# The next pass's expert routing gathered into fewer job slots in passes 1 and 2 of a two-layer expert kernel

## The chip, the cores and the metric

The kernel runs on one core of a Trainium2 chip. The metric is the device time of one execution in microseconds, as the median of several runs. Five engines work side by side, each through its own list of instructions in order, and wait for each other by semaphores: TensorE (PE), VectorE (DVE), ScalarE (ACT), GpSimd (POOL) and SyncE (SP, which only issues transfers here).

## The reference, cut to what matters

```python
x = x + attention(layernorm(x))          # 4 batches x 512 tokens x 128
x = x + experts(layernorm(x))            # expert layer 1
x = x + recurrent(layernorm(x))          # gated linear recurrence, convolutions of 4 taps
x = x + experts(layernorm(x))            # expert layer 2, same weights

def experts(x):                          # 2048 tokens, 8 experts, 128 -> 352 -> 128
    scores = softmax(x @ gate_w.T)
    sel = top_k(scores + expert_bias, 2)             # two experts for each token
    for each (token, expert): row = x[token] * scores[token, expert]
        out[token] += (silu(row @ w1[e]) * (row @ w3[e])) @ w2[e]
```

Which expert a token goes to must be worked out on the chip before its rows can be gathered by expert. This working out is called routing here.

## The kernel before

**Passes and jobs.** After the attention, both expert layers run as one stream of 92 jobs on all engines. The 2048 tokens are cut in two halves of 1024, so there are four passes: pass 0 and 1 are layer 1 on the first and the second half of the tokens, pass 2 and 3 are layer 2 on the same halves. A pass (`m` in the code) has `JOBS` = 23 jobs; a job is up to 128 gathered rows of one expert. Job `J` = 23 m + s stands in slot `s` of pass `m`; jobs 23 to 45 are pass 1, jobs 46 to 68 pass 2, jobs 69 to 91 pass 3.

**One job.** POOL fetches 128 rows by an indirect DMA (`gather_pool`, L1482, "fetch" below). PE turns them (L1538), ACT copies them out of PSUM (L1550, "copy"), PE multiplies them with w1 (L1568, into bank A) and w3 (L1571, into one of two banks B); these two are "the product" of the job below. ACT takes the silu of bank A (L1642), DVE multiplies it with bank B (`mix_vector`, L1709, "mix"), PE turns the result (L1534), ACT copies it, PE multiplies with w2 (L1584), ACT takes the result out (`take_out_scalar`, L1649, "take-out"), and POOL scatters it to DRAM (`return_pool`, L1490, "return"). The stages are staggered: in the slot of job J, PE does the product of J, turns the mix of J-1 and the rows of J+2, and multiplies J-2 with w2; ACT takes out J-2.

**Waits between neighbours.** There is one bank A: `up_tensor(J)` waits for the silu of J-1 (`s_silu`). Everything that stands ahead of that silu in ACT's list so delays PE's next product.

**What is done between the jobs.** After its part of the job of a slot, each engine does what a table gives that slot (`between_tensor`, `between_scalar`, `between_vector`, `between_pool`): adding the results of the pass before, norms, the recurrence, and the routing of the next pass, m+1. The table for passes 1 and 2 is `IN_LATER`, made by `later(first, scale)`, which adds `first` (3 in pass 1, 1 in pass 2) to each entry. The routing of pass m+1 consists of these stages:

- `logits`: PE, 16 small products (L1285). `softmax`: DVE takes the maximum and subtracts it (L1343, L1344). `exp`: ACT (L1308), with a table load before it and another before the next silu.
- `top`: DVE, sum, reciprocal, scaling, bias (L1347 to L1350). `first`, `second`: DVE, six instructions each, the first and the second expert of each token (L1355 to L1363); `second` ends with `chosen` and lets PE go on with `ranks`.
- `weigh`: DVE, the weights of the chosen experts (L1365, L1366). `ranks`: PE, two products with `chosen` (L1291, L1292), which wait for `second`.
- `slots`: DVE, nine instructions (L1373 to L1382), wait for `ranks`. `spread`: DVE, eight instructions (L1386 to L1397); ACT then does its part (`high`, L1311), which waits for the seventh of them, `injob`.
- `scale`: ACT, in two parts of eight instructions (L1320), the tokens times their weights; SP stores each part (L1469). The first waits for `weigh`. Where ACT has `high` and `scale` in one slot, `high` stands ahead.
- `lanes`: DVE, two instructions (L1403). `number`: PE, 16 products (L1300). `ids`, `experts`: DVE, the lists by which POOL fetches and by which PE picks the weights of a job.

Entries of `JOBS` = 23 or more are done behind the last job of the pass, up to `LAST_SLOT`.

**Behind the last job.** PE turns and multiplies what is left of the last jobs, ACT takes it out, POOL returns it. The fetches of pass 2 stand in POOL's list behind the return of the last job of pass 1 (job 45), nine at once; those of pass 3 begin behind the return of job 66, whose take-out stands in slot 22 (job 68) of pass 2, and alternate with the returns. When all returns of a pass have landed, SP loads the results back (`yb`, L1503, two transfers of 512 KB for passes 0 and 1 each), for the sums of the layer.

The order on an engine is the order of the calls; in a slot the job comes first and the routing behind it:

```python
def job_vector(J):
    ...
    mix_vector(J)
    between_vector(m, s)
```

Of the kernel before, what the change touches and what calls it, by code (L numbers as in the profile page):

```python
# [28 lines left out]
JOBS = 23  # L29
# [36 lines left out]
def build(nc, x, W, Wi, Wf, Wg, conv_i, conv_f, gnw, Wo, gate_w, ebias, w1, w2, w3, out):  # L66
# [8 lines left out]
    with ExitStack() as ctx:  # L75
# [175 lines left out]
        first = sb("first", [P, NE])  # L251
# [981 lines left out]
        def later(first, scale):  # L1233
            at = {'add x': (0, 1), 'stats x': (1, 2), 'apply x': (2, 3), 'turn x': (3, 4), 'project': (4, 6), 'taps': (4, 6),
                  'conv f': (4, 7), 'tanh': (5, 8), 'conv i': (5, 8), 'gate': (5, 8), 'silu': (6, 9), 'recur': (6, 9),
                  'squares': (7, 10), 'finish': (8, 10), 'means': (8, 10), 'out': (10, 11),
                  'stats y': (10, 12), 'apply y': (11, 13), 'turn y': (12, 14),
                  'logits': 15, 'softmax': 15, 'exp': 15, 'top': 16, 'first': 16, 'second': 17, 'ranks': 18, 'weigh': 17,
                  'scale': scale, 'slots': 18, 'spread': 19, 'lanes': (19, 20), 'number': 20, 'ids': 20, 'experts': 20,
                  'root x': (-2, -1), 'rms': (6, 8), 'root y': (8, 10)}  # L1240
            return {k: tuple(n + first for n in slots) if type(slots) is tuple else slots + first for k, slots in at.items()}

        IN_LATER = {1: later(3, (17, 18)), 2: later(1, (18, 19))}
        LAST_SLOT = {0: JOBS, 1: 24, 2: JOBS, 3: JOBS}
        ADDS_IN_LAST = (4, 5)


# [304 lines left out]
        experts = {}  # L1552
# [35 lines left out]
        def job_tensor(J):  # L1588
# [16 lines left out]
            if s == JOBS - 1:  # L1605
                turn_tensor_step(m, JOBS)
                down_tensor(J - 1)
                down_tensor(J)
                for s in range(JOBS, LAST_SLOT[m]):
                    between_tensor(m, s)  # L1610

        def between_tensor(m, s):
# [4 lines left out]
            elif m < 3:  # L1617
                at = IN_LATER[m]
                for k in range(2):
# [31 lines left out]
        def job_scalar(J):  # L1651
# [10 lines left out]
            if s == JOBS - 1:  # L1662
                turn_scalar_step(m, JOBS)
                take_out_scalar(J - 1)
                take_out_scalar(J)
                for s in range(JOBS, LAST_SLOT[m]):
                    between_scalar(m, s)

        def between_scalar(m, s):
# [4 lines left out]
            elif m < 3:  # L1674
                at = IN_LATER[m]
                for k in range(2):
# [46 lines left out]
        def between_vector(m, s):  # L1723
# [8 lines left out]
            elif m < 3:  # L1732
                at = IN_LATER[m]
                for k in range(2):
# [171 lines left out]
        def between_pool(m, s):  # L1906
# [3 lines left out]
            if m in (1, 2):  # L1910
                at = IN_LATER[m]
                for k in range(2):
# [166 lines left out]
```

## Time and profile before

| | |
|---|---|
| device time, median of 3 runs | 536.09 us (532.87 to 545.83) |
| span of the profiled execution | 534.2 us |
| PE, DVE, ACT, POOL busy in it | 427.9, 330.9, 333.2, 310.0 us |
| returns (L1490) on POOL | 92, 93.5 us busy, 52.4 us idle before them for ACT's take-out |
| mixes (L1709) on DVE | 92, 47.8 us busy, 83.8 us idle before them for PE's product |
| turns of fetched rows (L1538) on PE | 92, 10.8 us idle before them for the fetch |

Times in the trace count from the span's start. A row of a timeline has the start, the time on the engine, the line, the operation and its operands, and in brackets how long the engine was idle before it and what ended that. A row of a table of stretches has the stretch, its length, the busy time of each engine with the number of its instructions, and the granted clock of TensorE (1.00 is its upper level, 0.50 its lower).

### The profile page before, as it was taken

The numbers are of one execution on the slowest core, as the hardware profiler recorded it, in microseconds if no ns is written. First come the engines' busy times: TensorE is split into PE (matmuls) and PEld (weight loads), VectorE is DVE, ScalarE is ACT, GpSimd is POOL, SyncE is SP. The second block draws the span as 40 slices with busy tenths as digits, with TensorE's granted clock in tenths as the row PEclk, the third lists the DMA queues.
The fourth block names the chain that finished last, engine by engine and source line by source line (L and its number), as shares of the span: only waits on it lengthen the run. The fifth ranks groups of instructions, "written<-read, shape, count | busy, mean of one in ns | idle before, by whom it ended". The sixth has DMA issues, their size and how long they took to land. (4 is left out here: it accounts for less than half of the span.)

```text
span 534.2 us, 11420 instructions
## 1 busy us (share of the span) xinstructions
PE 427.9 (80%) x3805; PEld 321.2 (60%) x3822; DVE 330.9 (62%) x799; ACT 333.2 (62%) x624; POOL 310.0 (58%) x333
## 2 busy tenths in 40 slices
PE   3777798778787766998798798975799895699990
PEld 2455576556565554786576567753577774477770
DVE  5988889969957887154641678547377757132112
ACT  2486699899895868556754275564366565255550
POOL 5345385764663338676457576724567752667771
PEclk9796899999998679899999799897799998999996
DMA  7344353273369411112311312103311222151324
GB/s 156 82 110 92 89 115 74 79 141 55 88 158 293 100 42 42 41 45 43 113 41 49 109 50 37 34 21 117 106 34 44 38 40 95 36 162 51 56 51 128
DMA packets 36371, 43.50 MB, mean 81 GB/s; under 512 B 5876, under 2 KB 31276, under 8 KB 36292
## 3 DMA queue, kind: packets, MB, share of 16 engines
q1 hardware_dynamic: 30428, 30.70, 22.3%
q0 software_dynamic: 5888, 12.07, 9.2%
q8 instruction: 34, 0.56, 0.4%
q14 instruction: 21, 0.17, 0.1%
HBM read 25.91 MB, written 15.86 MB: 78 GB/s over the span
## 5 line engine op out<-in xcount | busy, mean ns | idle before, releaser
L1490 POOL DMA_INDIRECT token_out<-ysb,id_out x92 | 93.5, 1016 | 75.3 <-ACT ysb L1649 52.4
L1139 POOL TENSOR_TENSOR PP<-PP,E 128x512 f32<-128x512 f32 x64 | 83.1, 1299 | 72.9 <-ACT PP L1092 72.8
L1709 DVE TENSOR_TENSOR hid<-silu,ps 128x352 f32<-128x352 f32 x92 | 47.8, 519 | 114.6 <-PE ps L1571 83.8
L1092 ACT ACTIVATE PP<-A,feps 128x1024 f32<-128x1024 f32 x80 | 93.0, 1163 | 20.8 <-DVE A L1024 20.8
L1024 DVE TENSOR_SCALAR A<-ps 128x1024 int32<-128x1024 int32 x80 | 96.0, 1219 | 15.3 <-PE ps L923 14.0
L1482 POOL DMA_INDIRECT tiled<-scaled_rows,id_in x92 | 89.7, 975 | 26.7 <-issue 21.5
L1550 ACT ACTIVATE turned<-ps 128x512 f32<-128x512 f32 (+2 forms) x104 | 56.9, 547 | 67.8 <-PE ps L1538 63.7
L1568 PE MATMUL ps<-room,turned 128*128 x184 | 75.9, 495 | 11.4 <-ACT silu L1642 9.3
L1584 PE MATMUL ps<-room,turned 128*128 x552 | 79.8, 281 | 3.5 <-ACT ysb L1649 3.1
L1584 PEld LDWEIGHTS ps<-room,turned 128*128 128x128 f32 x552 | 70.8, 196 | 5.6 <-issue 5.2
L1571 PE MATMUL ps<-room,turned 128*128 x184 | 72.5, 477 | 0.0
L1642 ACT ACTIVATE silu<-ps 128x352 f32<-128x352 f32 x92 | 42.5, 462 | 38.6 <-PE ps L1568 38.5
L923 PE MATMUL ps<-QS,KS 102*128 102x128 bf16 (+2 forms) x448 | 53.6, 259 | 12.6 <-DVE A L1024 10.2
L1534 PEld LDWEIGHTS ps<-ident,hid 128*128 128x128 f32 x276 | 36.9, 146 | 28.8 <-issue 20.1
L923 PEld LDWEIGHTS ps<-QS,KS 102*128 102x128 bf16 x448 | 34.2, 105 | 27.5 <-DVE A L1024 11.2
L1534 PE MATMUL ps<-ident,hid 128*128 128x128 f32 x276 | 47.2, 282 | 3.5 <-DVE hid L1709 3.5
L1571 PEld LDWEIGHTS ps<-room,turned 128*128 128x128 f32 x184 | 36.3, 197 | 21.2 <-issue 2.8
L1101 ACT ACTIVATE E<-ps 128x512 f32<-128x512 f32 x64 | 38.4, 600 | 3.7 <-PE ps L953 3.6
L1568 PEld LDWEIGHTS ps<-room,turned 128*128 128x128 f32 x184 | 29.4, 199 | 16.4 <-issue 16.2
L1538 PE MATMUL ps<-ident,tiled 128*128 128x128 f32 x92 | 26.6, 289 | 12.1 <-DMA tiled<-scaled_rows,id_in 10.8
L1649 ACT ACTIVATE ysb<-ps 128x128 f32<-128x128 f32 x92 | 25.5, 277 | 15.0 <-PE ps L1584 10.5
L194 POOL TENSOR_TENSOR lnr<-lnv,mhalf 128x4 f32<-128x4 f32 x16 | 17.3, 1080 | 19.3 <-DVE lnv L188 19.3
(223 smaller groups left out, 640.9 us busy)
## 6 DMA issues: line engine op xcount, KB each, us to landing
parts<-room SPq DMA_DIRECT2D x32, 128.0 KB, 2.4
scaled_rows<-xT SPq DMA_DIRECT2D x8, 512.0 KB, 2.7
yb<-token_out SPq DMA_DIRECT2D x8, 512.0 KB, 4.2
QS<-parts SPq DMA_DIRECT2D x21, 192.0 KB
KS<-parts SPq DMA_DIRECT2D x21, 192.0 KB
room<-in_L_ffn_w_dram SPq DMA_DIRECT2D x2, 1408.0 KB, 8.1
tiled<-scaled_rows,id_in POOLq DMA_INDIRECT x92, 2.7
token_out<-ysb,id_out POOLq DMA_INDIRECT x92, 2.4
```

The lines of the kernel that those rows point to most:

```text
L923: return pe.matmul(bank[:, col:col + width], KS[:, slot, h, P * j:P * j + P], QS[:, slot, h, t0:t0 + width], start=True, stop=True)
L1024: v.tensor_scalar(A[:, U % 3, :].bitcast(I32), ps[:, bank:bank + 2, :].rearrange("p k t -> p (k t)").bitcast(I32), 0x7fffffff, None, ALU.b ...
L1092: a.activation(PP[:, G % 2, 2 * p:2 * p + 2, :].rearrange("p k t -> p (k t)"), A[:, U % 3, :], ACT.Square, bias=feps[:, G // NG:G // NG + ...
L1139: g.tensor_tensor(w, w, E[:, hh % 4, :], MUL).then_inc(s_PD, 1)
L1482: g.indirect_dma_start(rows[:, J % ROWS, :], None, xs_d[m], bass.IndirectOffsetOnAxis(ap=id_in[:, m % 2, s:s + 1], axis=0)).then_inc(s_row ...
L1490: g.indirect_dma_start(yr_d[m], bass.IndirectOffsetOnAxis(ap=id_out[:, m % 2, s:s + 1], axis=0), ysb[:, J % OUTS, :], None).then_inc(s_ret ...
L1534: ins = pe.transpose(ps[:, BK_R, P * c:P * c + P], hid[:, J % 2, P * c:P * c + P], ident[:, :])
L1550: a.activation(turned[:, n % 2, c0:c1, :].rearrange("p c l -> p (c l)"), ps[:, BK_R, P * c0:P * c1], ACT.Copy).then_inc(s_t, 1)
L1568: pe.matmul(ps[:, BK_A, 0:HID], turned[:, n % 2, 3, :], w13[:, bass.ds(e, 1), 0, :].squeeze(1), start=True, stop=True).then_inc(s_AB, 1)
L1571: pe.matmul(ps[:, BK_B + J % 2, 0:HID], turned[:, n % 2, 3, :], w13[:, bass.ds(e, 1), 1, :].squeeze(1), start=True, stop=True).then_inc(s_ ...
L1584: ins = pe.matmul(ps[:, BK_Y, 0:P], turned[0:hw, n % 2, c, :], w2s[0:hw, bass.ds(e, 1), c, :].squeeze(1), start=(c == 0), stop=(c == len(H ...
L1709: v.tensor_tensor(hid[:, J % 2, 0:HID], silu[:, J % 2, :], ps[:, BK_B + J % 2, 0:HID], MUL).then_inc(s_hid, 1)
```

## The change

In `IN_LATER` the stages of the routing stand in other slots. Slots of the job stream, with `first` added:

| stage | pass 1, before | pass 1, now | pass 2, before | pass 2, now |
|---|---|---|---|---|
| logits, softmax, exp | 18 | 18 | 16 | 16 |
| top, first | 19 | 18 | 17 | 16 |
| second, weigh | 20 | 19 | 18 | 17 |
| ranks | 21 | 19 | 19 | 17 |
| slots | 21 | 20 | 19 | 18 |
| spread, high | 22 | 20 | 20 | 18 |
| scale, two parts | 20, 21 | 20, 21 | 19, 20 | 18, 19 |
| lanes, two parts | 22, 23 | 21, 21 | 20, 21 | 19, 19 |
| number, ids, experts | 23 | 22 | 21 | 20 |

Nothing is left for slot 23 of pass 1, so its `LAST_SLOT` falls from 24 to 23. No instruction is added or removed, and the lists of POOL and SP are the same.

```diff
-                  'logits': 15, 'softmax': 15, 'exp': 15, 'top': 16, 'first': 16, 'second': 17, 'ranks': 18, 'weigh': 17,
-                  'scale': scale, 'slots': 18, 'spread': 19, 'lanes': (19, 20), 'number': 20, 'ids': 20, 'experts': 20,
+                  'logits': 15, 'softmax': 15, 'exp': 15, 'top': 15, 'first': 15, 'second': 16, 'ranks': 16, 'weigh': 16,
+                  'scale': scale, 'slots': 17, 'spread': 17, 'lanes': (18, 18), 'number': 19, 'ids': 19, 'experts': 19,
...
-        IN_LATER = {1: later(3, (17, 18)), 2: later(1, (18, 19))}
-        LAST_SLOT = {0: JOBS, 1: 24, 2: JOBS, 3: JOBS}
+        IN_LATER = {1: later(3, (17, 18)), 2: later(1, (17, 18))}
+        LAST_SLOT = {0: JOBS, 1: JOBS, 2: JOBS, 3: JOBS}
```

The first place is DVE in pass 1 behind the mix of job 41: the difference of the two lists, where L1343 and L1344 are the softmax stage, L1709 is the mix of job 42, and L1347 begins the stage `top`.

```order
 L1343 TENSOR_REDUCE m1<-ps 128x8
 L1344 TENSOR_TENSOR L8<-ps,m1 128x64
-L1709 TENSOR_TENSOR hid<-silu,ps 128x352
 L1347 TENSOR_REDUCE m1<-L8 128x8
 L1348 RECIPROCAL m1<-m1 128x8
```

The mix of job 42 now stands behind the stages `top` and `first`, ten instructions later in the list; pass 2 has the same difference at job 63.

The second place is PE around the `ranks` products (L1291, L1292) of pass 1. Before, they stood behind the w2 product of job 42 and ahead of the product of job 45, the last of the pass; the rows are those two and what follows them:

```order
 L1291 MATMUL ps<-chosen,trib 128x64
 L1292 MATMUL ps<-chosen,onesb 128x64
 L1568 ISA
 L1568 MATMUL ps<-room,turned 128x352
 L1571 ISA
 L1571 MATMUL ps<-room,turned 128x352
```

Now they stand behind the w2 product of job 40 (the rows L1584) and ahead of the product of job 43, whose `chosen` DVE works out in the same slot:

```order
L1584 MATMUL ps<-room,turned 128x128
L1291 MATMUL ps<-chosen,trib 128x64 [waits s_rd,s_M]
L1292 MATMUL ps<-chosen,onesb 128x64
L1568 ISA [waits s_silu,s_t]
L1568 MATMUL ps<-room,turned 128x352
```

So two whole jobs of PE (43 and 44) now stand behind these products that stood ahead of them.

The third place is ACT in pass 1 from the take-out of job 41 in slot 20 on: L1320 is a part of `scale`, L1642 the silu, L1311 the part `high`. Before:

```order
L1649 ACTIVATE ysb<-ps 128x128
L1320 ACTIVATE xT<-xh,wts 128x128 x8
L1642 ACTIVATE silu<-ps 128x352
L1550 ACTIVATE turned<-ps 128x384
L1649 ACTIVATE ysb<-ps 128x128
L1320 ACTIVATE xT<-xh,wts 128x128 x8
L1642 ACTIVATE silu<-ps 128x352
L1550 ACTIVATE turned<-ps 128x384
L1649 ACTIVATE ysb<-ps 128x128
L1311 ACTIVATE injobid<-injob,idhi 128x16x23
```

Now:

```order
L1649 ACTIVATE ysb<-ps 128x128
L1311 ACTIVATE injobid<-injob,idhi 128x16x23
L1320 ACTIVATE xT<-xh,wts 128x128 x8
L1642 ACTIVATE silu<-ps 128x352
L1550 ACTIVATE turned<-ps 128x384
L1649 ACTIVATE ysb<-ps 128x128
L1320 ACTIVATE xT<-xh,wts 128x128 x8
L1642 ACTIVATE silu<-ps 128x352
```

The part `high` has moved from behind both parts of `scale` and the silu of job 45 to ahead of the first part and of the silu of job 44. In pass 2 `high` stood ahead of the second part of `scale` and now stands ahead of the first.

## Rows read from the trace of the kernel before

**Rows 1.** Timeline of ACT, pass 1, slots 18 to 22 (start, us, instruction, idle before)
```profile
348.32 1.28 ACT L1308 ACT_TABLE_LOAD   x1
350.23 0.26 ACT L1308 ACTIVATE L<-L 128x64 f32<-128x64 f32 x1 [0.63 <-DVE L L1344]
...
357.79 2.44 ACT L1320 ACTIVATE xT<-xh,wts 128x128 f32<-128x128 f32 x8 [2.42 <-DVE wts L1366]
360.13 0.44 ACT L1642 ACTIVATE silu<-ps 128x352 f32<-128x352 f32 x1
...
363.34 0.45 ACT L1642 ACTIVATE silu<-ps 128x352 f32<-128x352 f32 x1
...
366.38 0.63 ACT L1311 ACTIVATE injobid<-injob,idhi 128x368 bf16<-128x368 bf16 x1 [1.16 <-DVE injob L1395]
...
368.74 0.28 ACT L1649 ACTIVATE ysb<-ps 128x128 f32<-128x128 f32 x1 [1.21 <-PE ps L1584]
```

**Rows 2.** Timeline of DVE, pass 1, slots 19 to 22
```profile
352.73 0.21 DVE L1347 TENSOR_REDUCE m<-L 128x8 f32<-128x64 f32 x1
...
355.29 0.52 DVE L1709 TENSOR_TENSOR hid<-silu,ps 128x352 f32<-128x352 f32 x1
...
357.00 0.23 DVE L1363 TENSOR_TENSOR chosen<-oh 128x64 bf16<-128x64 f32 x1
...
360.66 0.52 DVE L1709 TENSOR_TENSOR hid<-silu,ps 128x352 f32<-128x352 f32 x1 [2.91 <-ACT silu L1642]
...
363.18 0.27 DVE L1382 TENSOR_TENSOR base<-ps,cumE 128x64 f32<-128x64 f32 x1
...
364.32 0.29 DVE L1386 TENSOR_TENSOR Q<-oh,base 128x128 f32<-128x128 f32 x1
...
365.80 0.54 DVE L1395 TENSOR_TENSOR injob<-iojob,jobof 128x368 bf16<-128x368 f32 x1
```

**Rows 3.** Timeline of PE, products and ranks of pass 1
```profile
352.50 0.85 PE L1568 MATMUL ps<-room,turned 128*128 x2 [0.44 <-ACT silu L1642]
353.19 0.76 PE L1571 MATMUL ps<-room,turned 128*128 x2
...
354.89 0.76 PE L1568 MATMUL ps<-room,turned 128*128 x2
...
357.28 0.20 PE L1291 MATMUL ps<-chosen,trib 128*128 128x64 bf16 x1
...
360.82 1.54 PE L1568 MATMUL ps<-room,turned 128*128 x2 [3.30 <-ACT silu L1642]
```

**Rows 4.** Table of stretches: busy time of each engine, granted clock, DMA
```profile
357.40:360.70 3.30, 0.12 (x2) 0.00 (x0) 0.35 (x3) 2.92 (x10) 0.00 (x0) 1.00 0.03 6
360.80:364.10 3.30, 3.28 (x8) 2.18 (x9) 2.59 (x11) 3.00 (x11) 0.97 (x1) 0.50 0.45 179
```

**Rows 5.** Timeline, from pass 1 to pass 2: POOL, SP, PE
```profile
369.30 0.97 POOL L1490 DMA_INDIRECT token_out<-ysb,id_out  x1 [0.40 <-ACT ysb L1649]
371.19 0.98 POOL L1482 DMA_INDIRECT tiled<-scaled_rows,id_in  x1 [0.92 <-DVE id_in L1413]
...
371.80 0.80 SPq L1503 DMA_DIRECT2D yb<-token_out  x2
...
376.04 0.45 PE L1538 MATMUL ps<-ident,tiled 128*128 128x128 f32 x1 [6.42 <-DMA tiled<-scaled_rows,id_in]
```

**Rows 6.** Timeline, from pass 2 to pass 3: ACT, POOL, PE
```profile
433.24 0.26 ACT L1308 ACTIVATE L<-L 128x64 f32<-128x64 f32 x1 [0.63 <-DVE L L1344]
...
456.28 0.28 ACT L1649 ACTIVATE ysb<-ps 128x128 f32<-128x128 f32 x1 [0.79 <-PE ps L1584]
...
456.83 0.97 POOL L1490 DMA_INDIRECT token_out<-ysb,id_out  x1 [4.73 <-PE ps L1534]
458.11 0.98 POOL L1482 DMA_INDIRECT tiled<-scaled_rows,id_in  x1 [0.31 <-issue]
...
460.83 0.30 PE L1538 MATMUL ps<-ident,tiled 128*128 128x128 f32 x1 [1.61 <-DMA tiled<-scaled_rows,id_in]
```

## The prediction

> **What bounds the kernel now.** I first read the page for the share of each engine: none is full, PE is busiest with 80% of the span, so the job stream loses its time in waits and each stretch has to be read by itself. I then read the timelines of ACT, DVE and PE for slots 18 to 22 of pass 1 and 16 to 22 of pass 2, the only places that the change touches, and the waits of POOL and PE behind the last jobs.
>
> In [rows 1 to 3] the routing of pass 1 is seen to set the pace. The product of job 45 begins at 360.82, after PE was idle for 3.30 us [rows 3]. It waited for the silu of job 44 at 360.13, which stands in ACT's list behind the first part of `scale`, and that waited 2.42 us for the weights from DVE [rows 1]. The granted clock is 1.00 in that idle stretch and 0.50 in the next one, 2.4 and then 1.2 GHz [rows 4]; the first half of the product takes 1.54 us in place of 0.85 [rows 3].
>
> Between the passes the chain goes over transfers. The take-out of job 45 is at 368.74 [rows 1], its return at 369.30, and the fetch of job 46 only at 371.19, of which 0.92 us is a wait for the list `id_in` [rows 5]. PE can turn the fetched rows at 376.04, 4.85 us after the fetch began. The same step from pass 2 to 3 takes 2.72 us (458.11 to 460.83) [rows 6]. What differs is that SP begins to load 2 x 512 KB of results at 371.80, 0.61 us behind the fetch [rows 5].
>
> **What the change does to this.** I work out the new times in pass 1 from the instructions' own times, with before in brackets.
>
> 1. *Softmax to first choice.* Until the exponential, nothing moves: it ends at 350.49 [rows 1]. `top` and `first` then take 355.29 - 352.73 = 2.56 us on DVE [rows 2], so the mix of job 42 stands at 353.1. I price its own delay, about 0.8 us against a silu that ends near 352.3, at nothing as such, because PE turns it only in its next slot. What counts is what follows.
>
> 2. *`ranks` two jobs earlier.* `second` ends 357.23 - 355.29 = 1.94 us after the mix before it starts [rows 2], so at 355.0. PE has nothing left from 352.06 (the product at 352.50 less its 0.44 us idle) [rows 3]. The two `ranks` products stand ahead of the product of job 43 and are waited for now, where two jobs of work covered them before. With 0.05 us to begin and 0.2 us for them [rows 3], this product begins at 355.3 (352.50): **2.8 us late**. Queued behind it are the w2 product of job 41, its take-out and its return, and on DVE the mix of job 43, which needs bank B: 1.45 us after the product begins (353.19 + 0.76 - 352.50) [rows 3], at 356.75.
>
> 3. *`slots` and `spread` together, `high` ahead of `scale`.* From the mix to the end of `slots` it is 363.45 - 360.66 = 2.79 us, and to the end of `injob` another 366.34 - 364.32 = 2.02 us [rows 2]: 361.55. ACT waits for that with `high`, then 0.63 us for `high` and 2.34 us (360.13 - 357.79) for the first part of `scale` [rows 1]. The silu of job 44 begins at 364.5 (360.13): **4.4 us late**. PE is done with its work of the slot by about 360.1 (2.39 us for a job [rows 3], begun at 357.7) and idle until 365.1, again long enough for the lower clock, as before. The weights themselves are ready early now, which gains nothing, since `high` is ahead of their reader in the list.
>
> 4. *End of pass 1.* The silu of job 45 follows 3.21 us later (363.34 - 360.13) [rows 1], at 367.7 (363.34). `lanes` are done by then on DVE. Before, ACT's list still had `high` ahead of the last copies, and 5.40 us lay between this silu and the last take-out (368.74 - 363.34) [rows 1]. Now mix, turn, copy, w2 product and two take-outs follow in about 4.5 us: 372.2. That is **3.5 us late**, so four fifths of the 4.4 us remain.
>
> 5. *The fetch.* `ids` are long done, and the 0.92 us wait for them goes. The return of job 45 starts 0.56 us after its take-out and takes 1.27 us of POOL with the gap (458.11 - 456.83) [rows 5, 6]: the fetch starts at 374.0 (371.19), 2.8 us late. SP's loads begin 2.50 us after the start of the return (371.80 - 369.30) [rows 5], so 1.2 us behind the fetch now in place of 0.61. I take it that the fetch then keeps ahead of them and needs 2.72 us as in [rows 6], not 4.85 us. It may still need all of that; both ends go into the range. PE turns the rows at 376.75 (376.04): **0.7 us late**.
>
> 6. *Pass 2.* The list is the same one shifted by 433.24 - 350.23 = 83.01 us [rows 1, 6], up to the silu of job 65 at 447.5 and that of 66 at 450.7. The product of job 66 begins at 448.1 at the lower clock and lasts about 2.8 us (twice 1.45); with 1.4 us for the rest of the slot and 0.5 us for `number` the product of 67 begins at 452.8, that of 68 2.4 us later, and the take-out of 66 another 2.5 us behind: 457.7 (456.28), **1.4 us late** [rows 6]. The first fetch of pass 3 stands right behind the return of 66, so it is late by as much; it never waited for the lists, so their earlier slot gives nothing.
>
> The sum is 0.7 + 1.4 = 2.1 us on the profiled execution's 534.2 us, which gives 536.3. That execution lies 1.9 us below the median of the runs shown, 536.09, so I put the same 2.1 us on the median: **538.2 us**, 0.4% longer. Bounds: each of the two `ranks` waits leaves PE idle for some 3 us. If the clock falls to the lower level just as the late product begins, that costs the second 1.45 us of it [rows 3, 4]; both times, +2.9 us. If the fetch still needs 4.85 us, +2.1 us. Against this, if PE's idle time soaks up half of either delay, -1.8 and -0.7 us.
>
> Two rules of the Trainium skill can be held against these rows. The trace has the exponential 1.91 us after its table load began, and the 0.63 us idle before it was for DVE [rows 1]. The Trainium skill, page "ScalarE: Activation LUTs", section "What ACT_TABLE_LOAD costs", counts 1.28 us for the load and 1.38 us more for a drain, 2.66 us for each switch. By it the exponential could not begin before 350.98 and step 1 would end 0.75 us later in each pass; the trace, with the exponential at 350.23, does not agree. The other is on step 5. In the trace the same fetch takes 4.85 us with the loads 0.61 us behind it and 2.72 us without them [rows 5, 6]. The Trainium skill, page "DMA: Bandwidth & Descriptors", section "Queues, rings and completion order", says that a DMA engine takes turns between the queues that have work. By it the loads slow every fetch that is under way, whichever began first, and most of the 2.1 us would not come back; the trace shows a fetch slowed that began first, so this counts as a rival below.
>
> **Rivals.**
>
> - *The boundary pays for it (faster).* At the turn from pass 1 to 2 the change takes away 0.92 us of waiting for `id_in` and up to 2.13 us (4.85 - 2.72) of the fetch [rows 5, 6], 3.05 us in all. If the last take-out is late by less than 3.05 us the turn gains; if it is not late at all, because DVE's stages now fill time in which PE waited for ACT anyway (3.30 us idle at 360.82 [rows 3]), the kernel takes 536.1 - 3.05 = 533.0 us. For it: second choice and weights end 2.2 us sooner on DVE. Against it: `high` now holds ACT for `spread`.
> - *Clock and crowding (slower).* The waits of steps 2 and 3 come at the lower clock and the fetch stays slow: 538.2 + 2.9 + 2.1 = 543.2 us at most, 541 us with about half. For it: one idle stretch of this size in pass 1 has the clock at 0.50 right behind it [rows 4]. The rule on the DMA queues above is part of this case.
> - *Hidden anyway.* The late jobs wait for the same fetches and returns in the end, and only noise is left: 536.1 us. Against it: in the turn to pass 2 the fetches stand behind the last return in POOL's list, so the delay has no buffer to go into.
>
> **How the numbers follow.** The forecast, 536.5 to 540 us, has 0.45; clock and crowding, 540 to 543.5 us, 0.25; faster at the turn, 532.5 to 535.5 us, 0.2; hidden, around 536, 0.1. The range that leaves out no more than 2 in 10 reaches from 533.5 to 543.5 us. The two percent that a measurement of this kernel can tell from no change is 10.7 us; no case reaches it, and only the scatter of the runs (532.87 to 545.83) or something unseen would. So: faster 0.04, same 0.88, slower 0.08.
>
> **What would show it.** In the changed kernel's timeline PE should idle about 3 us before the `ranks` products in both passes; ACT should wait for `injob` (L1311) about 3 us before the first part of `scale`; POOL's 0.92 us for `id_in` should be gone; the first fetch of pass 2 should take under 3.5 us until PE turns it. Wrong would be the forecast if the last take-out of pass 1, measured from the exponential, comes less than 20.5 us behind it (18.5 before, 22.0 forecast), or if the first fetch takes over 4 us.

## The result and the profile after

The changed kernel takes 545.16 us (median of 4 runs, 543.99 to 545.28) against 537.38 us of the kernel before (4 runs, 532.87 to 545.83): ratio 1.0153, 95% interval 1.0116 to 1.019, so 7.8 us slower. Forecast were 538.2 us and a range up to 543.5 us. The direction came true and both waits are there; the size did not, and neither did what was said of the turn between the passes and of the clock. The forecast started from 536.09 us, the median of three runs; with a fourth the kernel before is at 537.38 us. Beside that the change cost 7.8 us, where 2.1 us were forecast.

The span of the profiled execution is 543.5 us (534.2 before). 1.3 us of that difference is there before the first moved instruction: the exponential of pass 1 ends at 351.79 and not at 350.49 [rows 1]. I therefore read everything from that exponential on. First the timeline of ACT in slots 18 to 22 of pass 1 (columns as before), which answers to [rows 1].

```profile
351.53 0.26 ACT L1308 ACTIVATE L<-L 128x64 f32<-128x64 f32 x1 [0.63 <-DVE L L1344]
...
357.47 0.46 ACT L1642 ACTIVATE silu<-ps 128x352 f32<-128x352 f32 x1 [3.25 <-PE ps L1568]
...
363.05 0.62 ACT L1311 ACTIVATE injobid<-injob,idhi 128x368 bf16<-128x368 bf16 x1 [2.62 <-DVE injob L1395]
363.57 2.42 ACT L1320 ACTIVATE xT<-xh,wts 128x128 f32<-128x128 f32 x8
365.89 0.44 ACT L1642 ACTIVATE silu<-ps 128x352 f32<-128x352 f32 x1
...
369.10 0.45 ACT L1642 ACTIVATE silu<-ps 128x352 f32<-128x352 f32 x1
...
372.96 0.28 ACT L1649 ACTIVATE ysb<-ps 128x128 f32<-128x128 f32 x1 [1.21 <-PE ps L1584]
```

ACT now waits 3.25 us for the late product of job 43 and 2.62 us for `injob` ahead of `scale`. From the exponential to the silu of job 44 it is 14.4 us (9.9 before), to the last take-out 21.4 us (18.5). PE in the same slots and in the turn to pass 2, as the work between the last job of one pass and the first of the next is called below, answering to [rows 3, 5]:

```profile
356.38 0.20 PE L1291 MATMUL ps<-chosen,trib 128*128 128x64 bf16 x1 [3.01 <-DVE chosen L1363]
...
356.58 0.85 PE L1568 MATMUL ps<-room,turned 128*128 x2
...
366.58 0.85 PE L1568 MATMUL ps<-room,turned 128*128 x2 [3.60 <-ACT silu L1642]
...
377.58 0.45 PE L1538 MATMUL ps<-ident,tiled 128*128 128x128 f32 x1 [4.66 <-DMA tiled<-scaled_rows,id_in]
378.48 1.53 PE L1568 MATMUL ps<-room,turned 128*128 x2 [0.45 <-ACT turned L1550]
...
382.00 0.45 PE L1538 MATMUL ps<-ident,tiled 128*128 128x128 f32 x1 [0.81 <-DMA tiled<-scaled_rows,id_in]
```

Both new waits are there. The first of them is followed by a product at the upper clock (0.85 us); the clock falls 1.5 us later. The first fetch of pass 2 is turned at 377.58; the second, at 382.00, is a wait that the kernel before did not have. The transfers of the turn, POOL and SP:

```profile
373.51 0.97 POOL L1490 DMA_INDIRECT token_out<-ysb,id_out  x1 [0.52 <-ACT ysb L1649]
374.79 0.99 POOL L1482 DMA_INDIRECT tiled<-scaled_rows,id_in  x1 [0.30 <-issue]
376.08 0.97 POOL L1482 DMA_INDIRECT tiled<-scaled_rows,id_in  x1 [0.30 <-issue]
...
376.03 0.80 SPq L1503 DMA_DIRECT2D yb<-token_out  x2
```

The wait for `id_in` (0.92 us in [rows 5]) is gone and the first fetch starts 1.24 us ahead of the loads. The second is issued 0.05 us behind them. The trace gives for the first and for the second, from issue to landing:

```profile
DMA to landing us min/median/max: 2.7/2.7/2.7
...
DMA to landing us min/median/max: 5.8/5.8/5.8
```

Pass 2 and the turn to pass 3, PE and ACT, answering to [rows 6]:

```profile
438.07 0.26 ACT L1308 ACTIVATE L<-L 128x64 f32<-128x64 f32 x1 [0.62 <-DVE L L1344]
...
442.91 0.20 PE L1291 MATMUL ps<-chosen,trib 128*128 128x64 bf16 x1 [3.00 <-DVE chosen L1363]
...
443.11 1.40 PE L1568 MATMUL ps<-room,turned 128*128 x2
...
453.56 0.44 ACT L1642 ACTIVATE silu<-ps 128x352 f32<-128x352 f32 x1
...
454.24 1.54 PE L1568 MATMUL ps<-room,turned 128*128 x2 [4.61 <-ACT silu L1642]
...
464.57 0.28 ACT L1649 ACTIVATE ysb<-ps 128x128 f32<-128x128 f32 x1 [0.18 <-PE ps L1584]
```

Here the product behind the `ranks` wait runs at the lower clock: 1.40 us for its first half, 0.85 us in pass 1. The table of stretches (length; busy time of PE, PEld, DVE, ACT, POOL; granted clock) shows where the clock is low:

```profile
357.90:361.30 3.40, 3.40 (x14) 2.89 (x13) 2.74 (x11) 0.91 (x3) 0.60 (x1) 0.51 0.02 5
375.10:388.60 13.50, 9.39 (x19) 5.19 (x20) 2.33 (x4) 2.82 (x7) 8.27 (x9) 0.50 0.41 125
443.30:446.60 3.30, 3.30 (x10) 2.18 (x10) 0.75 (x4) 0.48 (x2) 0.00 (x0) 0.50 0.03 5
453.60:460.30 6.70, 6.06 (x32) 4.65 (x33) 3.80 (x7) 4.59 (x15) 2.24 (x2) 0.50 0.42 168
470.60:477.40 6.80, 6.25 (x16) 3.58 (x15) 1.04 (x2) 1.98 (x5) 4.49 (x5) 0.50 0.18 54
```

The same table of the kernel before:

```profile
371.10:381.20 10.10, 4.32 (x9) 2.27 (x10) 1.48 (x5) 1.30 (x4) 7.62 (x8) 0.50 0.45 150
381.40:449.40 68.00, 61.26 (x372) 47.09 (x371) 48.73 (x144) 43.53 (x96) 40.38 (x40) 1.00 0.17 43
449.60:456.30 6.70, 4.99 (x23) 3.88 (x24) 4.22 (x13) 1.48 (x5) 1.72 (x1) 0.50 0.22 88
456.40:524.00 67.60, 58.39 (x337) 43.94 (x335) 14.58 (x27) 32.52 (x76) 48.23 (x49) 1.00 0.27 72
```

So in the turn to pass 2 the lower clock lasts 3.4 us longer now, and the stretches at 443 and 470 us have no counterpart before. The idle time of 3.60 us ahead of the product at 366.58 was not followed by the lower clock: from 361.4 to 374.9 us it is 1.00.

The stretches below are differences of start times in one trace each; `after_again` and `after_third` are two later traces of the changed kernel. "exp" is the exponential of the pass, "s44" the silu of job 44, "y45" the take-out of job 45; the take-outs y45 and y66 are those that the first fetches of the next pass hang on.

| kernel | exp to s44 | s44 to y45 | y45 to s46 | s46 to s49 | sum | exp to s65 | s65 to y66 | y66 to s69 | s69 to s72 | sum |
|---|---|---|---|---|---|---|---|---|---|---|
| before | 9.9 | 8.6 | 9.8 | 7.1 | 35.4 | 5.5 | 17.6 | 6.3 | 7.8 | 37.1 |
| changed | 14.4 | 7.1 | 7.1 | 10.5 | 39.1 | 15.5 | 11.0 | 6.6 | 8.9 | 42.1 |
| changed, `after_again` | 14.4 | 8.7 | 7.1 | 9.8 | 40.0 | 15.6 | 9.8 | 7.1 | 9.9 | 42.5 |
| changed, `after_third` | 14.4 | 8.8 | 7.1 | 10.0 | 40.2 | 15.6 | 8.7 | 7.2 | 9.6 | 41.1 |

Between s49 and the exponential of pass 2 the first two traces take 47.6 and 47.5 us, from s72 to the last take-out 51.0 and 50.9 us. So the loss behind the first exponential is in these columns, 3.7 us in the sum of pass 1 and 4.9 us in that of pass 2; only some 0.4 us of it comes back behind the last take-out. The single columns of the three traces of the changed kernel differ by up to 2.3 us (s65 to y66), which is to be kept in mind wherever one trace is compared with another.

### The profile page after: what moved, and what is told of

It reads as the page before. It is cut to its first block and busy times, and to the rows that moved or that the text cites. A ratio compares the mean times of both kernels' runs of the same rounds, so it can differ in the third digit from the quotient of the medians.

```text
span 543.5 us, 11435 instructions
## 1 busy us (share of the span) xinstructions
PE 437.7 (81%) x3822; PEld 325.6 (60%) x3822; DVE 329.9 (61%) x799; ACT 333.2 (61%) x624; POOL 312.0 (57%) x333
## 5 line engine op out<-in xcount | busy, mean ns | idle before, releaser
L1490 POOL DMA_INDIRECT token_out<-ysb,id_out x92 | 94.6, 1028 | 82.0 <-ACT ysb L1649 62.0
L1709 DVE TENSOR_TENSOR hid<-silu,ps 128x352 f32<-128x352 f32 x92 | 47.7, 518 | 119.8 <-PE ps L1571 97.1
L1568 PE MATMUL ps<-room,turned 128*128 x184 | 78.8, 512 | 14.5 <-ACT silu L1642 12.5
L1584 PE MATMUL ps<-room,turned 128*128 x552 | 80.0, 282 | 2.5 <-ACT ysb L1649 2.2
L1571 PE MATMUL ps<-room,turned 128*128 x184 | 74.7, 490 | 0.0
L1584 PEld LDWEIGHTS ps<-room,turned 128*128 128x128 f32 x552 | 71.0, 196 | 4.3 <-issue 4.0
L1642 ACT ACTIVATE silu<-ps 128x352 f32<-128x352 f32 x92 | 42.5, 461 | 44.3 <-PE ps L1568 44.2
L923 PE MATMUL ps<-QS,KS 102*128 102x128 bf16 (+2 forms) x448 | 54.0, 260 | 11.2 <-DVE A L1024 8.8
L1534 PEld LDWEIGHTS ps<-ident,hid 128*128 128x128 f32 x276 | 36.8, 146 | 30.1 <-issue 20.8
L1571 PEld LDWEIGHTS ps<-room,turned 128*128 128x128 f32 x184 | 37.7, 205 | 22.6 <-issue 5.3
L1568 PEld LDWEIGHTS ps<-room,turned 128*128 128x128 f32 x184 | 30.3, 205 | 19.2 <-issue 18.9
L1101 ACT ACTIVATE E<-ps 128x512 f32<-128x512 f32 x64 | 38.4, 600 | 3.1 <-PE ps L953 2.9
L1649 ACT ACTIVATE ysb<-ps 128x128 f32<-128x128 f32 x92 | 25.5, 277 | 15.5 <-PE ps L1584 11.0
```

The lines of the kernel that those rows point to most:

```text
L923: return pe.matmul(bank[:, col:col + width], KS[:, slot, h, P * j:P * j + P], QS[:, slot, h, t0:t0 + width], start=True, stop=True)
L1490: g.indirect_dma_start(yr_d[m], bass.IndirectOffsetOnAxis(ap=id_out[:, m % 2, s:s + 1], axis=0), ysb[:, J % OUTS, :], None).then_inc(s_ret ...
L1534: ins = pe.transpose(ps[:, BK_R, P * c:P * c + P], hid[:, J % 2, P * c:P * c + P], ident[:, :])
L1568: pe.matmul(ps[:, BK_A, 0:HID], turned[:, n % 2, 3, :], w13[:, bass.ds(e, 1), 0, :].squeeze(1), start=True, stop=True).then_inc(s_AB, 1)
L1571: pe.matmul(ps[:, BK_B + J % 2, 0:HID], turned[:, n % 2, 3, :], w13[:, bass.ds(e, 1), 1, :].squeeze(1), start=True, stop=True).then_inc(s_ ...
L1584: ins = pe.matmul(ps[:, BK_Y, 0:P], turned[0:hw, n % 2, c, :], w2s[0:hw, bass.ds(e, 1), c, :].squeeze(1), start=(c == 0), stop=(c == len(H ...
```

## The experiments

My theory was: PE's waits for `ranks` and for the silu behind `high`, with the lower clock that they bring, make the loss (A). Rivals: it is made in the turn, by SP's loads ahead of the second fetch (B); only `high` ahead of `scale` counts (C) or only `ranks` (D). The experiments ran on three chips. On two of them (chips 7 and 13) the kernel before takes 537.4 and 537.6 us, as in the first comparison, whose chip is not known. On chip 6 it takes 570 to 573 us; no trace of it was kept there, but every kernel traced there takes longer outside the routing (52.4 to 56.2 us from s49 to the exponential of pass 2). Ratios are to the kernel before on the same chip, with 95% intervals. The stretches can be compared over chips in part: with the old table in pass 1, `pass2_only` on chip 6 has 9.9, 8.6, 9.8 and 7.1 us as the kernel before has above, and `exp to s44` of the changed kernel is 14.4 us in all its traces; where the lower clock plays in, they scatter by 1 to 2 us.

**Undoing one list edit each.** `ranks_later`:

```diff
-'second': 16, 'ranks': 16, 'weigh': 16,
+'second': 16, 'ranks': 17, 'weigh': 16,
```

> The changed kernel with one entry put back: ranks stands one slot behind second again, all other stages stay where the change put them. Theory A (PE's waits, and the lower clock behind them, make the loss; changed kernel 545.2 us): the 3.0 us idle time ahead of L1291 goes in both passes, the mixes of jobs 43 and 64 come 1.2 to 2.5 us sooner, and the granted clock no longer falls right behind that wait; about 541 us. Rival B (the loss is made in the turn from pass 1 to 2, where SP's 2 x 512 KB loads stand ahead of the second and third fetch): the turn still costs its 3.5 us, only the direct 1.2 us of each pass come back; about 543 us. Rival C (only the lists' order on ACT counts, high ahead of scale): no more than 1 us, 544 us.

Measured on chip 6: 1.0051 (1.0007 to 1.0095), 575.1 us beside 572.5 us, near the 541 us of theory A.

`high_later` leaves the table and moves ACT's part one slot later and behind `scale`:

```diff
-            if s == at["spread"]:
-                prepare_scalar(m + 1, "high")
             for k in range(2):
                 if s == at["scale"][k]:
                     scale_scalar(m + 1, k)
+            if s == at["spread"] + 1 and m:
+                prepare_scalar(m + 1, "high")
```

> The changed kernel, only ACT's part high (L1311) of passes 1 and 2 moved to the slot behind, after the second part of scale, so that the silu of jobs 44 and 65 no longer waits for injob. Theory A: the silu of jobs 44 and 65 comes about 3 us sooner, PE's idle time of 3.60 and 4.61 us ahead of the next product falls to 1 to 2 us; 2.5 to 3 us come back in each pass, about 539.5 us. Rival B: the delay of the last take-out shrinks, but the second fetch of pass 2 is still behind the loads; about 541 us. Rival D (the ranks wait alone is what counts, and high is hidden by it): 544 to 545 us.

Measured: 0.9974 (0.9927 to 1.0022), 573.1 us. `both_later` has both:

> The changed kernel with both edits: ranks one slot later, and high behind scale in the slot behind. Theory A: both waits gone, about 536 us, level with the kernel before or 1 us below it. Rival B: the turn from pass 1 to 2 still costs 3 us, about 539 us.

Measured: 0.9936 (0.9884 to 0.9989), 567.5 us; repeated on chip 13 as `both_later_2`:

> The changed kernel with ranks one slot later and high behind scale, as both_later, now beside the others on one chip. By its stretches 3.2 us better than the kernel before in passes 1 and 2 together, ratio 0.992 to 0.996; so 9 to 12 us better than the changed kernel. If the two list edits only trade with the clock, 0.998 or more.

Measured: 0.9893 (0.9857 to 0.9929), 531.9 us beside 537.6 us, and 12.8 us below the changed kernel on that chip, somewhat more than expected. The stretches:

| kernel | exp to s44 | s44 to y45 | y45 to s46 | s46 to s49 | sum | exp to s65 | s65 to y66 | y66 to s69 | s69 to s72 | sum |
|---|---|---|---|---|---|---|---|---|---|---|
| ranks_later | 13.0 | 8.7 | 7.1 | 10.1 | 38.9 | 13.0 | 10.7 | 7.0 | 8.1 | 38.7 |
| high_later | 11.4 | 7.6 | 7.0 | 10.0 | 36.0 | 12.3 | 9.2 | 7.1 | 8.0 | 36.6 |
| both_later | 7.7 | 10.7 | 7.1 | 10.4 | 35.9 | 8.6 | 10.2 | 7.2 | 7.4 | 33.4 |
| both_later_2 | 7.7 | 10.7 | 7.1 | 10.6 | 36.0 | 7.7 | 10.7 | 7.1 | 9.3 | 34.7 |

`exp to s44` falls by 1.4, 3.0 and 6.7 us, `exp to s65` by 2.5, 3.2 and 6.9 to 7.8 us: both waits are real, each is partly hidden behind the other, and in these stretches the two together are worth more than their sum. In the times they are not: against the changed kernel on chip 6 (1.0127) they gain 0.8%, 1.5% and together 1.9%, with intervals of 0.5% each. That `high_later` alone is level with the kernel before excludes D. C is excluded less firmly: `ranks_later` lies 0.8% below the changed kernel, just beyond the noise, and its take-outs y45 and y66 come 1.4 and 1.7 us nearer to the exponentials than in the trace of the changed kernel on that chip; of the two, `high` ahead of `scale` weighs more. `high_later` came out much better than the 539.5 us that I had expected by theory A, level with the kernel before. In the timeline of ACT of `both_later_2` one sees why the pair wins:

```profile
349.94 0.26 ACT L1308 ACTIVATE L<-L 128x64 f32<-128x64 f32 x1 [0.63 <-DVE L L1344]
...
355.28 2.45 ACT L1320 ACTIVATE xT<-xh,wts 128x128 f32<-128x128 f32 x8 [0.20 <-DVE wts L1366]
357.64 0.44 ACT L1642 ACTIVATE silu<-ps 128x352 f32<-128x352 f32 x1
...
358.51 2.44 ACT L1320 ACTIVATE xT<-xh,wts 128x128 f32<-128x128 f32 x8
360.84 0.62 ACT L1311 ACTIVATE injobid<-injob,idhi 128x368 bf16<-128x368 bf16 x1
```

The weights are ready when ACT comes to `scale` (0.20 us of waiting, 2.42 us in [rows 1]), and `high` finds `injob` done.

**The stage that the change is named for, alone.** `top_first_only` is the kernel before with `top` and `first` moved into the logits' slot:

```diff
-'top': 16, 'first': 16,
+'top': 15, 'first': 15,
```

> The kernel before with one part of the change alone: top and first moved into the slot of the logits, ahead of the mix of jobs 42 and 63; second, weigh, ranks and all later stages as before. In the traces this part by itself delays one mix by 0.8 us that PE does not need yet, and it makes the next mix 1.7 us sooner. If the waits for ranks and high make the loss, this part costs nothing: ratio to the kernel before 0.998 to 1.002, the silu of job 44 at most 0.3 us off. If the mix put behind DVE's ten instructions is what costs, 1 to 2 us slower and a later silu 44.

Measured on chip 7: 0.9957 (0.9912 to 1.0001), 536.6 us beside 537.4 us; exp to s44 is 8.7 us (9.9), 1.2 us less where 0.3 us at most was expected. The mix that DVE does later is not missed. The wait of DVE for the exponential ahead of the mix shows no cost; this part of the change is at worst neutral.

**The two passes apart.** `pass1_only` and `pass2_only` give the old entries to the other pass.

```diff
-        IN_LATER = {1: later(3, (17, 18)), 2: later(1, (17, 18))}
+        IN_LATER = {1: later(3, (17, 18)), 2: later(1, (18, 19), True)}
```

This is `pass1_only`, where `True` puts the old entries into the table; `pass2_only` has it the other way round, with the old `LAST_SLOT`.

> The new table in pass 1 alone, pass 2 as before. By the first traces the changed kernel loses 3.5 us up to slot 3 of pass 2 (the turn included) and 4.8 us from the routing of pass 2 on. So this one should be 3.5 us (2.5 to 4.5) slower than the kernel before. If the second fetch behind SP's loads is the main cause, most of the 8 us is here.

> The new table in pass 2 alone, pass 1 as before: 4.8 us (3.5 to 6) slower than the kernel before, no wait for SP's loads being involved. If the turn from pass 1 to 2 is the main cause, 1 to 2 us only.

> The changed kernel itself once more, beside the others on one chip, as the measure for them: ratio to the kernel before 1.012 to 1.019 if the first comparison holds on any chip; theory and rivals agree on it. If a chip with slower transfers hides the loss in its own waits, the ratio is below 1.01.

Measured on chip 6: 1.0141 (1.0092 to 1.019), 1.0054 (1.001 to 1.0099), and 1.0127 (1.007 to 1.0183) for the whole change; by the medians that is 6.9, 3.3 and 7.2 us. The two parts add up to more than the whole, within the intervals. It is not the split that I had expected (3.5 and 4.8 us), and by the times alone most of the loss is in pass 1, as rival B would have it. The stretches decide:

| kernel | exp to s44 | s44 to y45 | y45 to s46 | s46 to s49 | sum | exp to s65 | s65 to y66 | y66 to s69 | s69 to s72 | sum |
|---|---|---|---|---|---|---|---|---|---|---|
| pass1_only | 14.7 | 7.7 | 7.1 | 10.0 | 39.3 | 5.5 | 17.2 | 6.4 | 9.3 | 38.4 |
| pass2_only | 9.9 | 8.6 | 9.8 | 7.1 | 35.4 | 15.6 | 10.6 | 6.9 | 7.2 | 40.4 |

Pass 1 costs 3.9 us, and 3.8 us of that are there at the take-out of job 45. The turn behind it, y45 to s49, takes 17.0 us with the new table and 16.9 us with the old one. So the loss is not made in the turn: the turn only fails to give back what the prediction had counted on. Pass 2, which has no such loads, costs 2.0 us here (40.4 against 38.4), or 3.2 us against the kernel before. B is thereby excluded as the maker of the loss.

**The clock without the waits.** `fill_all` and `fill_waits` leave every wait and give PE products to do in it that nobody reads. The edit of `fill_waits`:

```diff
+        def fill_tensor(n):
+            for _ in range(n):
+                nc.tensor.transpose(ps[:, BK_F, 0:P], ident[:, :], ident[:, :])
...
+                    fill_tensor(26)
                 pe.wait_ge(s_M, m + 1)
...
+            if m in (1, 2) and s == IN_LATER[m]["spread"] + 2:
+                fill_tensor((0, 30, 38)[m])
```

> The changed kernel with turns of a constant tile on PE, into a PSUM bank that is free there, that nobody reads: 26 ahead of ranks, 28 ahead of the product of jobs 45 and 66, 38 ahead of the first fetched rows of pass 2 and 12 ahead of those of pass 3 (0.11 us each at the upper clock). They do no useful work and move no wait, they only keep PE busy. Theory A with the clock as the larger part: the granted clock stays at 1.00 in slots 19 to 22 of pass 1 and 17 to 20 of pass 2 and behind both turns, and 4 to 6 us of the 8 us come back, about 540 us. If the clock is only a by-product: no change or some tenths slower, 545 to 546 us.

Measured on chip 6: 1.0078 (1.0036 to 1.012). It settles nothing: its second filling stood one slot too early (`spread` + 1), and between the passes it had 38 more ahead of the fetched rows. There, from the take-out of job 45 to the silu of 46, it took 11.2 us in place of 7.1. So I made `fill_waits`, in the two waits alone:

> The changed kernel with PE kept busy by products that nobody reads in its two waits alone: 26 ahead of ranks in passes 1 and 2 (3.0 us of waiting there), 30 ahead of the product of job 45 and 38 ahead of that of job 66 (3.6 and 4.6 us of waiting there); nothing in the turns between the passes. No wait is moved. If the lower clock behind the waits is the larger part of the loss, 3 to 5 us come back against the changed kernel run beside it and the granted clock stays at 1.00 through these slots. If the waits alone count, the difference is under 1 us.

Measured on chip 6: 1.0097 (1.0056 to 1.0138) beside 1.0127 of the changed kernel, too close to tell. Repeated on chip 13 with more executions:

> The changed kernel once more beside the two below, with more rounds: 1.013 to 1.016 of the kernel before, whichever theory holds.

> The changed kernel with PE kept busy by products nobody reads in its two waits (as fill_waits). Earlier traces have it 1.6 us better than the changed kernel in pass 1 and 4.2 us in pass 2, the times only 0.3% (2.4 us less, intervals of 4 us). If the clock holds the larger part of the loss as those traces say: 4 to 6 us better than the changed kernel, ratio to before 1.003 to 1.008. If the clock is the smaller part: 1.009 to 1.012.

Measured: the changed kernel 1.014 (1.0106 to 1.0175), with fillings 1.0067 (1.0036 to 1.0098), 544.7 and 540.4 us. The difference of 0.0073 is 3.9 us, with the two intervals together uncertain by about 2.5 us; on chip 6 it was 0.003. So a part of the loss, by the better of the two measurements about half, is the clock behind the waits, and the rest is left with the clock mostly held up there. The timeline of PE in `fill_waits_2` (L1279 is the filling, L1576 the first half of the product):

```profile
354.76 0.20 PE L1299 MATMUL ps<-chosen,trib 128*128 128x64 bf16 x1 [0.16 <-DVE chosen L1371]
...
354.97 0.85 PE L1576 MATMUL ps<-room,turned 128*128 x2
...
359.55 3.44 PE L1279 MATMUL ps<-ident 128*128 128x128 f32 x30
364.98 0.85 PE L1576 MATMUL ps<-room,turned 128*128 x2 [1.99 <-ACT silu L1652]
```

The idle time ahead of `ranks` is 0.16 us in place of 3.01, and these products are at the upper clock. Beside the trace of the changed kernel on the same chip, `after_third`:

| kernel | exp to s44 | s44 to y45 | y45 to s46 | s46 to s49 | sum | exp to s65 | s65 to y66 | y66 to s69 | s69 to s72 | sum |
|---|---|---|---|---|---|---|---|---|---|---|
| after_third | 14.4 | 8.8 | 7.1 | 10.0 | 40.2 | 15.6 | 8.7 | 7.2 | 9.6 | 41.1 |
| fill_waits_2 | 14.4 | 7.7 | 7.1 | 10.0 | 39.1 | 14.4 | 8.7 | 7.0 | 7.7 | 37.8 |

The fillings give back 1.1 us in pass 1, ahead of the last take-out, and 3.3 us in pass 2, more than half of it not before the first jobs of pass 3 (s69 to s72). In pass 1 the lower clock lasts 3.2 us (366.2 to 369.4) in place of 6.6 us (369.4 to 376.0 in `after_third`); the turn to pass 2 runs at the lower clock for 13.4 or 13.5 us in both.

**The turn.** `hold_loads` is the changed kernel with SP's loads held back until PE has turned the third fetch:

```diff
+            if m == 1 and b % 2 == 0:
+                sp.wait_ge(s_tp, turns(2 * JOBS + 2))
             sp.dma_start(yb[:, b % 2], ...)
```

> The changed kernel, SP's two loads of pass 1's results (yb, 2 x 512 KB) held back until PE has turned the rows of job 48, the third fetch of pass 2; nothing else moved. If the loads ahead of the second and third fetch are the reason why job 46 to 49 took 10.0 to 10.5 us (silu of 46 to silu of 49) in place of 7.1 us, this falls by 1 to 2 us, though the sum with yb then comes later (its DVE part may give some of it back); 1 to 2 us better than the changed kernel. If only the lower clock is the reason, the stretch stays at 9.5 to 10.5 us.

Measured on chip 7: 1.0148 (1.009 to 1.0206), no gain. Silu of 46 to silu of 49 is 7.7 us where the three traces of the changed kernel have 9.8 to 10.5, so the loads did cost 2 to 3 us there. A part of that is clock: the lower level lasts 6.7 us in this turn (378.8 to 385.5) in place of 13.5. But the gain is given back: from s49 to the exponential of pass 2 it is 49.9 us in place of 47.5, since DVE now waits for the results that it adds and holds the mix behind them (timeline of DVE, the wait in brackets):

```profile
388.05 0.69 DVE L1511 TENSOR_TENSOR yb<-yb 128x512 f32<-128x512 f32 x1 [1.65 <-DMA yb<-token_out]
388.78 0.69 DVE L1512 TENSOR_TENSOR xt<-xt,yb 128x512 f32<-128x512 f32 x1
389.39 0.51 DVE L1711 TENSOR_TENSOR hid<-silu,ps 128x352 f32<-128x352 f32 x1
```

`early_two` moves two fetches in front instead, between the returns of jobs 44 and 45:

```diff
-            return (J - ROWS, max(17 + s // 2, J - 9), max(2 * JOBS - 1, J - 9), ...)[m]
+            return (J - ROWS, max(17 + s // 2, J - 9), 2 * JOBS - 2 if s < 2 else max(2 * JOBS - 1, J - 9), ...)[m]
```

> The changed kernel, and POOL issues the first two fetches of pass 2 between the returns of jobs 44 and 45, not behind that of 45: possible only because the lists are now ready by then. The first fetch starts about 1.5 us sooner, the loads 2.5 us later, three fetches land before the loads take the DMA engines. Last take-out of pass 1 to silu of job 49: 17.6 us in the changed kernel, 16.8 before; here 14.5 to 15.5 us, so 2 to 3 us better than the changed kernel. If the clock alone sets that stretch, 17 us and no gain.

Measured on chip 7: 1.0116 (1.0041 to 1.0191), not told apart from the changed kernel by its times, so the 2 to 3 us expected do not show there. In the trace y45 to s49 is 14.7 us (5.6 + 9.1) in place of 16.9 to 17.6, as expected, and s49 to the next exponential stays at 47.5: nothing given back. The same trace has 8.8 us from s44 to y45, where the lower clock lasts from 367.7 to 374.6 us; the first trace of the changed kernel has 7.1 us there at the upper clock, its two repetitions 8.7 and 8.8 us. So this term depends on where the clock falls in each run.

**All together.** `best` has both list edits, the two early fetches, and the fetches of pass 3 one return sooner (`3 * JOBS - 4` in place of `3 * JOBS - 3`).

> Both list edits (ranks one slot later, high behind scale) and the fetches issued sooner, the first two of pass 2 between the returns of 44 and 45 and those of pass 3 one return sooner. From the parts: the two list edits alone gave 0.9936 of the kernel before; the early fetches should give 2 to 3 us at the first turn and 1.5 us at the second. Ratio 0.984 to 0.990. If the turns are bound by the clock or by the loads anyway, 0.993 as without them.

Measured on chip 7: 0.9773 (0.9731 to 0.9815), 525.0 us (524.3 to 527.1) beside 537.4 us, 12 us faster than the kernel before and more than I had added up. Its stretches are 7.7, 9.6, 5.0, 8.9 (31.2) and 7.7, 10.7, 4.5, 7.3 (30.1). POOL in the turn to pass 2:

```profile
370.17 0.99 POOL L1482 DMA_INDIRECT tiled<-scaled_rows,id_in  x1 [0.30 <-issue]
371.46 0.96 POOL L1482 DMA_INDIRECT tiled<-scaled_rows,id_in  x1 [0.30 <-issue]
372.72 1.00 POOL L1490 DMA_INDIRECT token_out<-ysb,id_out  x1 [0.31 <-issue]
```

And the table of stretches of `best` from 4.1 us behind the silu of job 46 past the turn to pass 3:

```profile
379.50:461.00 81.50, 72.23 (x434) 54.58 (x433) 54.41 (x160) 49.36 (x111) 52.58 (x52) 1.00 0.19 53
```

The early fetches to pass 2 are possible only because the lists are ready before the last return; in the kernel before, POOL still waited for `id_in` behind it. Without them `both_later_2` was 1.1% faster than the kernel before, so the new table is worth having by itself once the two stages are moved. The clock holds its upper level from 379.5 us through the routing of pass 2 and the turn to pass 3, where the kernel before had 6.7 us of the lower one. `both_later_2`, without the early fetches, has the lower clock there again (456 to 466 us), and `early_two`, without the list edits, from 453 to 460 us; why the two together escape it is not shown.

## Why the prediction was wrong

- **Steps 1 and 2 held.** `ranks` was waited for 3.01 and 3.00 us; with the 1.3 us by which the traces differ beforehand taken off, the product of job 43 was 2.8 us late, as worked out, and in pass 2 the product of 64 began at 438.28 on the time axis of before (forecast 438.3).
- **Step 3 held.** The silu of job 44 was 5.76 - 1.3 = 4.5 us late (forecast 4.4).
- **Step 4 held in its sign.** The last take-out was 4.22 - 1.30 = 2.9 us late (forecast 3.5) in this trace; in the two repetitions of the changed kernel it comes 23.1 us behind the exponential, where before has 18.5, so 4.5 and 4.6 us late: nothing of the 4.4 us was soaked up there.
- **Step 5 is where it failed first.** It had the turn give back 2.8 us, from 3.5 us late at the take-out to 0.7 us late at the turned rows. The first fetch did escape the loads and landed in 2.7 us, as said, and its rows were turned 0.2 us late. But I priced the turn by the first fetch alone. The second, issued 0.05 us behind SP's loads, took 5.8 us and PE had to wait 0.81 us for it, and the lower clock lasted 3.4 us longer; before, the first fetch took that blow and the second, 5.1 us under way, landed while PE was busy with the first job. By s49 the loss was 3.7 us, not 0.7 us: from y45 to s49 it is 16.9 us before and 17.6, 16.9 and 17.1 us in the three traces of the changed kernel, so the turn gave nothing back. `hold_loads` shows the loads' share with the clock in it (2 to 3 us of that stretch), `early_two` that moving fetches ahead of them wins it without giving it back. The "2.13 us gained" was moved to the next fetch.
- **Step 6 failed in the clock.** The product of job 64 began when forecast and then ran at the lower clock: its mix came at 441.06 on the time axis of before, against 439.75 by the steps. I had that price, 1.45 us, in the bounds and left it out of the sum, though the mix behind it is in the chain. In this trace y66 was 3.5 us late (forecast 1.4), in the repetitions 2.4 and 1.3 us. From y66 to s72, which I had at nothing, another 1.4 us are lost here and 2.9 and 2.7 us in the repetitions; but two kernels with the scale and `ranks` of pass 2 where they were before, `pass1_only` and `top_first_only`, have 9.3 and 9.6 us from s69 to s72 as well, where the kernel before has 7.8 us in its one trace. So this last part can't be put down to the change with certainty.
- **The range.** Its upper end allowed 1.45 us of clock for each of two waits and 2.1 us for the fetch, 5.0 us in all. The measured 545.16 us lie 1.7 us above it, of which 1.3 us is the start value (536.09 us of three runs, 537.38 us of four). The case "clock and crowding" was the nearest one and had a quarter of the chance, but the fetch that it let stay slow was the first, and that one was fast.
- **The signs.** All that was named as a sign came true: the idle time ahead of `ranks`, ACT's wait for `injob` (2.62 us), no wait for `id_in`, the first fetch under 3.5 us, the take-out beyond 20.5 us. None of them looked at the second fetch or at the clock, where the forecast failed.
- **Of the two rules weighed.** That of the Trainium skill on a table load (page "ScalarE: Activation LUTs", section "What ACT_TABLE_LOAD costs") did not hold here either: in the changed kernel the exponential again begins 1.91 us behind its table load (349.62 to 351.53), with 0.63 us of idle time for DVE, and DVE goes on 0.03 us after it ends. That of the Trainium skill on DMA engines taking turns between queues (page "DMA: Bandwidth & Descriptors", section "Queues, rings and completion order") should have had more weight: the traces agree with it for a fetch that shares its time with the loads (4.85 us before, 5.8 us now). The first fetch of the changed kernel, issued 1.24 us ahead of them, began 28 of its 32 packets before the first packet of the loads (376.4 to 377.0 us), so it had hardly anything to share; before, with 0.61 us between them, the loads' packets began at 372.6 and the fetch's at 374.0 us.

What stays open: how the 7.8 us divide between the waits themselves, the clock behind them and the turn is known only to some 2 us, as the traces of the changed kernel differ by as much in single stretches; why the clock falls behind one wait and not behind another of the same length; and the 1.3 us before the first moved instruction.

## What to carry to other kernels

In lists that run in order, moving a stage into the slot of the stage that feeds it can turn a covered hand-over into a wait of every engine behind it, as here; keep a slot of other work between producer and consumer, and put a part that waits behind those that do not. When a stall ahead of PE is priced, price the lower clock behind it as well, and compare several traces, since it does not fall in the same place each time. When a transfer is moved out of the way of another, follow the second and third in the queue, not only the first; and let a stage that is finished early pay by issuing its first transfer early.

## What the runs showed of the hardware

An indirect fetch of 128 rows takes 2.5 to 2.8 us from issue to landing alone, and up to 5.9 us when 1 MB of direct loads is under way. Its time goes with how far ahead of the loads it is issued: 1.24 us ahead it took 2.7 us (changed kernel; 2.5 and 2.6 us in `early_two` and `best`), 0.83 us ahead 3.8 us (`top_first_only`), 0.61 us ahead 4.7 us (before), 0.05 us behind them 5.8 us (changed kernel).

The granted clock does not follow PE's idle time alone. Behind the 3.00 us ahead of `ranks` in pass 2 the next product was at the lower level in the changed kernel's first and third traces (1.40 and 1.53 us). Behind the same 3.0 us in pass 1 it was at the upper one (0.85 us in all three traces); in the first the clock fell 1.5 us later, in `after_third` it stayed at 1.00 until the next wait, of 5.26 us. A wait of 3.60 us in the first trace was not followed by the lower level, one of 3.30 us in the kernel before was. With PE kept busy by products that nobody reads the same waits cost 3.9 us less (1.014 against 1.0067 of the kernel before, each uncertain by 0.3%). Chip 6 ran the same kernel in 570 to 573 us in place of 537 us.
